# A running maximum in a fused Perceiver kernel: one reduction over three columns, with the difference and the copy moved to a later step

## The reference

```python
q, k, v = x @ Wq + bq, y @ Wk + bk, y @ Wv + bv      # 16 heads of 32; y is the context
attn = softmax(q @ k.T / sqrt(32))                   # 512 x 8192 for each head
x = x + relu(attn @ v @ W1 + b1) @ W2 + b2
x = x + mamba_block(layernorm(x))                    # scan over 16 states, then an FFN
x = x + quantised_lora_ffn(layernorm(x))
```

## Time and profile before

| | |
|---|---|
| Median of 3 runs | 3216.33 us (3213.32 to 3224.85) |
| The profiled execution: its time, its span | 3226.74 us, 3224.9 us |
| TensorE busy | 3062.7 us, 95% of the span |
| VectorE busy | 2261.7 us, 70% |
| GpSimd busy | 1944.0 us, 60% |
| ScalarE busy | 1695.5 us, 53% |
| Granted TensorE clock, mean over the span | 0.978 |

### The profile page before, as it was taken

The page is one execution under the profiler, slowest core; times in us unless marked ns, Lnnn a source line. Parts: engine busy times, 40 slices in busy tenths (PEclk is TensorE's granted clock), DMA queues, the critical chain, the costliest instruction groups (busy, mean ns, idle before and its releaser), DMA issues.

```text
span 3224.9 us, 41368 instructions
## 1 busy us (share of the span) xinstructions
PE 3062.7 (95%) x15384; PEld 1834.8 (57%) x15384; DVE 2261.7 (70%) x3635; ACT 1695.5 (53%) x2967; POOL 1944.0 (60%) x490
## 2 busy tenths in 40 slices
PE   7899999999999999999999999999979877799999
PEld 4566666666666666666666666666524333344477
DVE  7677777777777677777777777777726799995753
ACT  1566665666666566666666666666631546330121
POOL 1588887988888787888889788888850000000000
PEclk9999999999999999999999999999989988899999
DMA  5422232232223233232223222322131112124100
GB/s 154 120 50 70 65 80 60 60 74 70 70 50 80 64 93 90 62 83 59 70 55 90 60 60 67 77 70 50 45 125 51 40 52 105 52 79 158 66 14 17
DMA packets 100684, 230.14 MB, mean 71 GB/s; under 512 B 22850, under 2 KB 27970, under 8 KB 99234
## 3 DMA queue, kind: packets, MB, share of 16 engines
q1 hardware_dynamic: 100484, 227.49, 25.8%
HBM read 114.46 MB, written 8.06 MB: 38 GB/s over the span
## 4 chain that ended last, share of the span: by engine, by line
PE 82%; DVE 13%; issue 2%; ACT 1%; POOL 1%; DMA 1%; SPq 0%; ACTq 0%; DVEq 0%; POOLq 0%
PE ps L1753 15%; PE ps L1714 15%; PE ps L1740 12%; PE ps L1667 9%; PE ps L1698 9%; PE ps L1691 6%; DVE pm L979 6%; PE ps L1939 4%; PE ps L1765 3%; PE ps L1903 3%; PE ps L1919 2%; DVE bx L1215 1%; PE ps L1726 1%; PE ps L1722 1%; DVE bx L1161 1%
## 5 line engine op out<-in xcount | busy, mean ns | idle before, releaser
L979 DVE TENSOR_REDUCE pm<-ps 128x1 f32<-128x512 f32 x2048 | 1406.8, 691 | 653.4 <-PE ps L1714 580.8
L1439 ACT ACTIVATE pf<-ps 128x512 f32<-128x512 f32 x2048 | 1215.1, 600 | 809.6 <-PE ps L1740 735.0
L837 POOL TENSOR_TENSOR psum<-psum,pf 128x2048 f32<-128x2048 f32 x256 | 1176.5, 4596 | 140.0 <-ACT pf L1439 128.5
L1714 PE MATMUL ps<-ks,qs 96*128 96x512 f32 x2048 | 855.5, 418 | 26.3 <-DVE pm L979 24.1
L1740 PE MATMUL ps<-qs,ks 98*128 98x512 f32 x2048 | 815.7, 399 | 2.9 <-ACT pf L1439 2.7
L837 POOL TENSOR_TENSOR psum<-pf 128x2048 f32<-128x2048 f32 x128 | 585.9, 4577 | 212.8 <-ACT pf L1439 212.7
L1714 PEld LDWEIGHTS ps<-ks,qs 96*128 96x128 f32 x2048 | 387.7, 189 | 316.7 <-issue 213.1
L1753 PE MATMUL ps<-pf,V 128*32 128x512 f32 x4096 | 495.4, 601 | 0.0
L1740 PEld LDWEIGHTS ps<-qs,ks 98*128 98x128 f32 x2048 | 391.7, 191 | 51.4 <-ACT pf L1439 12.2
L845 POOL PARTITION_ALL_REDUCE qstat<-qstat x2 | 0.7, 365 | 643.5 <-DVE qstat L1251 643.5
L1691 PE MATMUL ps<-cTh,Wkg 128*128 128x512 f32 x732 | 296.4, 405 | 21.9 <-issue 18.7
(11 more groups left out here) (212 smaller groups left out, 3099.2 us busy)
## 6 DMA issues: line engine op xcount, KB each, us to landing
ks<-KH SPq DMA_DIRECT2D x512, 128.0 KB, 2.4
ks<-KL SPq DMA_DIRECT2D x256, 128.0 KB, 2.4
cT<-in_ctxT SPq DMA_DIRECT2D x32, 768.0 KB, 5.0
Wkg<-wk_rows SPq DMA_DIRECT2D x61, 384.0 KB, 3.3
BC<-bc_rows SPq DMA_DIRECT2D x32, 512.0 KB, 4.8
ring<-in_ffn_w SPq DMA_DIRECT2D x16, 1024.0 KB, 5.4
wA<-in_W_fcT SPq DMA_DIRECT2D x4, 1024.0 KB, 10.0
wB<-in_W_projT SPq DMA_DIRECT2D x4, 1024.0 KB, 6.9
```

The costliest lines, as they stand in the source:

```text
L837: pool.tensor_tensor(acc, before, pf[:, tile % P_SLOTS, :], ALU.add).then_inc(s_sum, 1)
L979: dve.tensor_reduce(pm[:, n // BLK, n % BLK:n % BLK + 1], src, AX.X, ALU.max).then_inc(s_wfree, 1)
L1439: act.activation(pf[:, tile % P_SLOTS, j * NTOK:(j + 1) * NTOK], ps[:, S_BANK + u % S_BANKS, :], ACT.Exp, scale=SCALE).then_inc(s_exp, 1)
L1714: last = pe.matmul(dst, qs[0:3 * HD, h, t * P:(t + 1) * P], ks[0:3 * HD, keys_of(of, j), i * 512:(i + 1) * 512], start=True, stop=True)
```

## The change

`pm` gets a third column per pair, which holds the running maximum of the coming group. `new_max` becomes one reduction over the three columns and the negation. The difference, the copy to `m_run`, its reset in the last chunk, and a new copy that puts the next group's running maximum into the third column become `keep_max`, called on VectorE at the end of step 32 (step 0 of the group itself), and in the lead-in right behind `new_max`. `shrink` on ScalarE goes to the end of step 32 as well.

```diff
-        pm = sb("pm", [P, HG * NT, BLK], c=att)
-        mc = sb("mc", [P, HG * NT], c=att)
+        pm = sb("pm", [P, HG * NT, BLK + 1], c=att)
...
             dve.memset(m_run[:], LOWEST)
+            dve.memset(pm[:, :, BLK], LOWEST)
...
             def new_max(x, of):
-                n_fin = of * 3
-                def fin_link(ins, i):
-                    ins.then_inc(s_fin, 1)
-                    dve.wait_ge(s_fin, n_fin + i)
+                dve.wait_ge(s_wfree, work_count(x) + WORK_BANKS)
+                dve.tensor_reduce(mn[:], pm[:], AX.X, ALU.max).then_inc(s_fin, 1)
+                dve.wait_ge(s_fin, of + 1)
+                dve.tensor_scalar(nm[:], mn[:], -1.0, None, ALU.mult).then_inc(s_nm, 1)
+
+            def keep_max(of):
                 g = of % NG
                 r = slice(g * HG * NT, (g + 1) * HG * NT)
-                dve.wait_ge(s_wfree, work_count(x) + WORK_BANKS)
-                fin_link(dve.tensor_reduce(mc[:], pm[:], AX.X, ALU.max), 1)
-                fin_link(dve.tensor_tensor(mn[:], mc[:], m_run[:, r], ALU.max), 2)
-                dve.tensor_scalar(nm[:], mn[:], -1.0, None, ALU.mult).then_inc(s_nm, 1)
                 dve.tensor_tensor(dm[:], m_run[:, r], mn[:], ALU.subtract).then_inc(s_dm, 1)
                 dve.wait_ge(s_dm, of + 1)
-                fin_link(dve.tensor_copy(m_run[:, r], mn[:]), 3)
+                dve.tensor_copy(m_run[:, r], mn[:]).then_inc(s_kept, 1)
+                dve.wait_ge(s_kept, of + 1)
                 if of // NG == NCH - 1:
                     dve.memset(m_run[:, r], LOWEST).then_inc(s_reset, 1)
                     dve.wait_ge(s_reset, g + 1)
+                if of + 1 < NGT:
+                    g = (of + 1) % NG
+                    dve.tensor_copy(pm[:, :, BLK], m_run[:, g * HG * NT:(g + 1) * HG * NT]).then_inc(s_seed, 1)
+                    dve.wait_ge(s_seed, of + 1)
...
                 if pieces is None:
                     empty(x)
+                    if x == ("A", HG * A_UNITS - 1):
+                        keep_max(0)
...
                 for x in work_at(i):
                     empty(x)
+                if i % UPG == 0 and 0 < i < UNITS:
+                    keep_max(i // UPG)
...
-                for x in work_at(i):
-                    if x[0] == "M":
-                        shrink(x[1])
+                if i % UPG == 0 and 0 < i < UNITS:
+                    shrink(i // UPG)
```

More of the change, by code:

```diff
@@ L322, in emit @@
         s_fin = sem("s_fin")
+        s_kept = sem("s_kept")
+        s_seed = sem("s_seed")
         s_dm = sem("s_dm")
```

## The result

| | before | after |
|---|---|---|
| Median | 3218.42 us (3213.32 to 3224.85, 5 runs) | 3529.17 us (3522.57 to 3533.78, 5 runs) |
| Ratio | | 1.0963, 95% interval 1.0945 to 1.098 |
| Span of the profiled execution | 3224.9 us | 3527.3 us |
| Mean granted clock | 0.978 | 0.935 |

What follows compares the result with a forecast made beforehand. TensorE, busy 95%, sets the pace, with VectorE late at new_max. Waits of 82 + 105 + 84 us plus 44 clock minus 36 gain give 279 us over 3216.3: 3495 us, range 3260 to 3590 (own case 3430 to 3580).

Steps and rivals of the forecast that it cites:

- The gain, 36 us: At new_max, three instructions leave, so TensorE's A matmul no longer waits for VectorE: 60 groups x 0.60 us saved.
- Cover at step 32, by busy time: VectorE idles 1.83 us during TensorE's burst; the three moved instructions need 0.63 us, so they cost nothing.
- The instructions with all operands in SBUF wait for GpSimd: At step 32, each moved VectorE instruction waits until GpSimd's running instruction is over, up to 4.6 us; chance 0.50.
- Who goes next: At step 32, GpSimd's next instruction gets in first, so each waits anew: 2.9, 7.2 or 6.15 us late by group kind.
- The clock, 44 us: TensorE drops to half clock after waits, 1.4 us for some 7 matmuls, in half of 63 groups (0 to 88 us).
- only the difference waits: Rival at step 32: the copies run beside GpSimd undelayed; 3300 to 3345 us, say 3320; chance 0.26.
- nothing waits: Rival at step 32: all three run beside GpSimd undelayed, the busy-time count holds; 3180 us (3172 to 3190); chance 0.17.
- a slice of an add is enough: Rival at step 32: the three wait, but only for part of a GpSimd add; 3190 to 3260 us; chance 0.07.

Runs made afterwards that it cites:

- kernel with reductions: Changed kernel with the difference and both copies of keep_max at step 32 written as reductions with one SBUF input: 3183.73 us, ratio 0.9878 to the kernel before.
- kernel with the difference alone: Changed kernel with the two copies as reductions over one column, the difference still a two-input instruction: 3370.47 us, ratio 1.0457 to the kernel before.
- kernel with the copies alone: Changed kernel with the difference as a reduction over two columns, both copies from SBUF to SBUF kept: 3364.64 us, ratio 1.0434 to the kernel before.
- half adds: Changed kernel with every GpSimd add cut into two of 1024 columns: 3423.4 us, ratio 1.0617 to the kernel before.
- short delay: Kernel with reductions plus 3 idle VectorE reductions ahead of the difference at step 32: 3224.17 us, ratio 1.0003 to the kernel before.

## Why the prediction was right, step by step

- **The gain, 36 us.** Right. The kernel with reductions has it alone: 3222.17 - 3183.73 = 38 us, and TensorE's wait for the A bank is gone from its waits. It was worked out from one group's five starts and the count of groups.
- **Cover at step 32, by busy time.** Right: where nothing contends, the three fit into the burst. 1.39 us are left where 1.83 - 0.63 gives 1.20; 0.08 us of the rest is that the difference starts before the record of the reduction ahead of it ends (1020.98 for 1021.06). The reset stands in 4 groups (28 to 31) and not in 8, which changes nothing here.
- **The instructions with all operands in SBUF wait for GpSimd.** Right, for both forms. The forecast rested on a gap in the rows: 64 of 64 in pauses. What fills the gap is now measured. But the step said too much when it said that the trace has no VectorE instruction with two SBUF inputs beside a running GpSimd instruction. The lead-in of the kernel before has seven:

```profile
15.23 1.86 POOL L800 MEMSET Oacc<- 128x2112 f32 x1 [6.26 <-DVE xq L898]
15.52 1.76 DVE L954 TENSOR_TENSOR Wkl<-Wk,Wkh 128x1536 fp32r<-128x1536 f32 x1 [0.42 <-ACT Wkh L1399]
17.14 7.08 POOL L803 MEMSET ks<- 2x4096 f32 x2
17.20 1.89 DVE L948 TENSOR_TENSOR cTl<-cT,cTh 128x512 fp32r<-128x512 f32 x3
```

  They do not wait: 512 columns take 0.68 or 0.69 us, no more than an A reduction of 512. GpSimd's instruction is a memset there, which reads no tile; at step 32 it is an add, a split or a rescale, which read SBUF. So the wait is shown for these and not for every GpSimd instruction. Whether it is the reading that makes the difference was not tried. The Trainium skill's rule ("SBUF — State Buffer", "Who interferes with whom") holds in each part that was tried: a VectorE instruction with two SBUF inputs waits out a GpSimd add (4.20 us), and a reduction does not (0.18 us). A copy from SBUF to SBUF waits too (4.00 us); the rule says this of a copy in a two-port mode, and the trace does not show a copy's mode. The runs show which forms wait, not that ports are the reason.
- **Who goes next.** This step failed in its size: "GpSimd's next instruction gets in first, so each may wait anew". It gets in 0.13 us after its last, and the first copy is 0.03 us behind the difference, so it passes; only the seed copy, 0.24 us behind, waits anew. VectorE is late, against 1.99 us for on time, by 5.8 us (7.2 forecast) where `of % 4` is 1 and by 4.6 us (6.15) where it is 2, by 2.7 us (2.9) in plain groups. In plain groups TensorE loses 2.15 or 2.54 us of that (2.5 forecast), where `of % 4` is 1 it loses 5.65 (7.0), where it is 2, 4.07 (5.6). The waits were to be 82 + 105 + 84 = 271 us; the row says 215.1 us, and since a record lasts 0.165 us beyond the next possible start, 68 times, 226 us.
- **The clock, 44 us.** Too small. 3529.17 - 3183.73 = 345 us, less 226 leaves about 120 us. The granted clock says the same: in groups 1 to 62 it is at the lower level for 328 us, 66 of them while TensorE waits anyway, and half of the other 262 us is 131 us. Both parts of the term were too small. I took the loss for half of the groups, and the clock fell in 54 of the 62, in all 31 with a long wait (3.4 to 5.5 us) and in 22 of the 30 plain ones up to group 60. And I took 7 matmuls at half clock; in group 21 there are 14, from 960.32 to 966.44. The kernel with the difference alone shows the fall behind a plain group's wait too (its A matmuls in group 23):

```profile
982.99 0.50 PE L1722 MATMUL ps<-ks,qs 96*128 96x512 f32 x1 [2.34 <-DVE pm L981]
983.79 0.40 PE L1722 MATMUL ps<-ks,qs 96*128 96x512 f32 x1
984.85 0.63 PE L1722 MATMUL ps<-ks,qs 96*128 96x512 f32 x1
```

- The two sizes, 45 us too much and some 76 too little, nearly cancel: 3495 for 3529. The sum is better than its terms.
- **The rivals.** That only the difference waits is refuted by the kernel with the copies alone, that nothing waits by the rows after the change, that a slice of an add is enough by the half adds: the wait scales with the length of the one instruction.

How GpSimd and VectorE settle who begins is inferred from starts and ends. What happens when both ask at once was not tried.

## What to carry to other kernels

Before moving a small VectorE instruction out of a busy stretch, look at what GpSimd does at the new place, not only at VectorE's idle time (the waits measured here were all for GpSimd instructions that read SBUF); 16 columns cost 0.17 us or 4.20 us by that alone. If it must stand beside GpSimd, write it as a reduction with a single SBUF input (a difference is a sum over two columns, a copy a reduction over one). An instruction with one input in PSUM and one in SBUF did not wait either: in the kernel before, the addition of the burst's result to `Oacc` (L999, 512 columns) takes 0.69 us in the 62 groups in which it lies wholly beside a GpSimd instruction, and 0.69 us in the one in which none runs. When an instruction has only been measured in another engine's pauses, its duration is not known elsewhere; check this by comparing starts over all repetitions.

## What was not expected of the hardware

- In the kernel with the difference alone, TensorE's clock fell to the lower level in or behind its wait of 2.34 us in 25 of 30 groups, and with the wait of 1.97 us in 10 of 15; in the 15 groups without a wait it never did. The kernel before, with 0.34 us idle in nearly every group, and the one with the short delay, with 0.49 us in every second, have a mean of 1.00 between 200 and 2200 us. In the changed kernel the late VectorE costs about one and a half times the wait: 345 us for 226.
- The turn goes by hundredths of a microsecond: a copy 0.06 us ahead of GpSimd's instruction passed, one 0.07 us behind waited 3.38 us.
- Busy time hides it. VectorE's share rose from 70% to 73% as its work stayed the same; only the mean duration of a group of instructions gives it away.
